# A small clear on GpSimd ahead of every gather of two graph convolutions

## The reference, cut to what matters

```python
def _gcn_conv(x, src, dst, W, b):
    ones = jnp.ones((src.shape[0],), x.dtype)
    deg_out = jnp.maximum(jax.ops.segment_sum(ones, src, num_segments=N), 1.0)
    deg_in = jnp.maximum(jax.ops.segment_sum(ones, dst, num_segments=N), 1.0)
    h = x * (deg_out ** (-0.5))[:, None]
    h = h @ W
    m = jax.ops.segment_sum(h[src], dst, num_segments=N)
    return m * (deg_in ** (-0.5))[:, None] + b

h = _gcn_conv(x, src, dst, W1, b1)
h = jax.nn.relu(h)
h = _gcn_conv(h, src, dst, W2, b2)
h = _layer_norm(h, gamma, beta)
```

## Time and profile before

| what | value |
|---|---|
| median of 3 runs | 5543.09 us (5528.74 to 5544.08) |
| span of the profiled execution, first to last instruction | 5492.7 us |
| median less that span | 50.4 us |
| busy share of the span: PE, PEld, DVE, ACT, POOL | 70%, 53%, 42%, 38%, 52% |
| mean granted TensorE clock | 0.822 of full speed |
| first convolution, first gather to last sum | 2793.8 to 4003.6 us |
| second convolution, first gather to last sum | 4074.4 to 5390.7 us |

### The profile page before, as it was taken

The page is one execution under the profiler, slowest core; times in us unless marked ns, Lnnn a source line. Parts: engine busy times, 40 slices in busy tenths (PEclk is TensorE's granted clock), DMA queues, the critical chain, the costliest instruction groups (busy, mean ns, idle before and its releaser), DMA issues. The chain is left out here.

```text
span 5492.7 us, 62308 instructions
## 1 busy us (share of the span) xinstructions
PE 3840.4 (70%) x14678; PEld 2895.6 (53%) x14678; DVE 2333.7 (42%) x6705; ACT 2062.8 (38%) x4818; POOL 2835.2 (52%) x2849
## 2 busy tenths in 40 slices
PE   4555577777769699999925555555566777777775
PEld 2333355555558588888813333333344555555554
DVE  7444455656546711111133233333354444444445
ACT  6333222222225522222243333333344555555552
POOL 2666655565540033333346666666626666666660
PEclk7776788889889899999957666777687888888987
DMA  3333466656568534444453333333323333333331
GB/s 106 103 108 105 142 190 188 197 176 203 186 211 278 180 104 108 113 113 107 97 164 97 98 96 97 98 98 98 96 89 92 90 91 89 88 89 89 90 89 57
DMA packets 329290, 674.18 MB, mean 123 GB/s; under 512 B 63069, under 2 KB 142237, under 8 KB 328812
## 3 DMA queue, kind: packets, MB, share of 16 engines
q0 software_dynamic: 146768, 365.78, 22.9%
q1 hardware_dynamic: 178716, 301.28, 18.1%
q10 hardware_dynamic: 3456, 3.15, 0.2%
HBM read 512.51 MB, written 165.30 MB: 123 GB/s over the span
## 5 line engine op out<-in xcount | busy, mean ns | idle before, releaser
L732 POOL DMA_INDIRECT messages<-work,small x880 | 888.4, 1010 | 637.1 <-ACT work L855 282.7
L782 POOL DMA_INDIRECT work<-conv_rows,tables x880 | 836.6, 951 | 549.2 <-issue 242.0
L2224 PE MATMUL bank<-work,reg_a 128*128 x1760 | 658.2, 523 | 604.9 <-issue 519.4
L772 POOL DMA_INDIRECT work<-conv_rows,tables x831 | 785.7, 946 | 448.6 <-issue 238.2
L2078 PE MATMUL bank<-reg_b,reg_a 128*128 x1760 | 580.0, 466 | 462.6 <-issue 219.3
L2224 PEld LDWEIGHTS bank<-work,reg_a 128*128 128x128 f32 x1760 | 416.2, 257 | 846.9 <-issue 786.3
L855 ACT ACTIVATE work<-bank,tables 128x256 f32<-128x256 f32 x880 | 399.3, 474 | 1083.8 <-PE bank L2078 672.1
L2370 PE MATMUL bank<-work,reg_a 128*128 128x256 f32 x1760 | 553.7, 442 | 285.2 <-DVE reg_b L1899 150.4
L1677 DVE TENSOR_TENSOR reg_b<-reg_b,bank 128x257 f32 x880 | 372.6, 423 | 837.3 <-remote 290.6
L2078 PEld LDWEIGHTS bank<-reg_b,reg_a 128*128 128x128 f32 x1760 | 356.1, 224 | 650.6 <-issue 612.1
L1899 DVE TENSOR_TENSOR reg_b<-reg_b,bank 128x256 f32 x880 | 371.3, 422 | 718.1 <-PE bank L2370 286.7
(11 more groups left out here) (457 smaller groups left out, 5304.1 us busy)
## 6 DMA issues: line engine op xcount, KB each, us to landing
reg_b<-messages SPq DMA_DIRECT2D x350, 258.0 KB
reg_a<-in_L_ffn_W_dram SPq DMA_DIRECT2D x56, 1024.0 KB
b_rows<-messages SPq DMA_DIRECT2D x116, 258.0 KB
reg_a<-item_rows SPq DMA_DIRECT2D x110, 256.0 KB
work<-conv_rows,tables POOLq DMA_INDIRECT x1711
work<-messages SPq DMA_DIRECT2D x98, 258.0 KB
messages<-work,small POOLq DMA_INDIRECT x880
conv_rows<-work SPq DMA_DIRECT2D x14, 896.0 KB, 4.1
```

The lines of the kernel that those rows point to most:

```text
L732: g.indirect_dma_start(msgs, bass.IndirectOffsetOnAxis(ap=PIDX[:, i % 32:i % 32 + 1], axis=0), G[:, u, :], None, bounds_check=BASES[2] + L ...
L772: g.indirect_dma_start(GC[:, u, 0:D], None, table, bass.IndirectOffsetOnAxis(ap=BSRC[:, b_:b_ + 1], axis=0)).then_inc(z(f"conv_in{u // 4}" ...
L782: g.indirect_dma_start(GC2[:, u, :], None, table, bass.IndirectOffsetOnAxis(ap=source_rank(i), axis=0)).then_inc(z(f"conv_in{u // 4}"), 16)
L2224: pe.matmul(ps[i % 8][:, 0:D + 1], OHP[:, i % OHR, :], GCf[:, bass.ds(offs[i % 4], D + 1)], start=True, stop=True).then_inc(z(f"{tag}_mm"), 1)
```

## The change

Ahead of each gather of both convolutions GpSimd now clears sixteen columns of `JUNK` and counts that in a new semaphore, `paced`. The clear itself waits until the clear of the gather before is complete. The gathers, their tables, their rings and their waits for free slots are the same, only that the wait for slots now stands with the clear.

```diff
@@ -769,6 +769,9 @@
                     u = b_ % UC
                     if b_ >= UC and b_ % 4 == 0:
                         pool.wait_ge(z(f"{tag}_free"), b_ - UC + 4)
+                    if b_:
+                        pool.wait_ge(z("paced"), b_)
+                    g.memset(JUNK[:, 0:16], 0.0).then_inc(z("paced"), 1)
                     g.indirect_dma_start(GC[:, u, 0:D], None, table,
                                          bass.IndirectOffsetOnAxis(ap=BSRC[:, b_:b_ + 1], axis=0)
                                          ).then_inc(z(f"conv_in{u // 4}"), 16)
@@ -779,6 +782,8 @@
                     u = i % U2
                     if i >= U2 and i % 4 == 0:
                         pool.wait_ge(z("p2_mm"), i - U2 + 4)
+                    pool.wait_ge(z("paced"), NBLK + i)
+                    g.memset(JUNK[:, 0:16], 0.0).then_inc(z("paced"), 1)
                     g.indirect_dma_start(GC2[:, u, :], None, table,
                                          bass.IndirectOffsetOnAxis(ap=source_rank(i), axis=0)
                                          ).then_inc(z(f"conv_in{u // 4}"), 16)
```

## The result

The changed kernel takes 5551.84 us (median of 20 runs, 5535.05 to 5573.52), the kernel before, beside it, 5538.88 us (20 runs, 5521.24 to 5555.96). The ratio is 1.0032, with a 95% interval of 1.0022 to 1.0042: slower by 0.3%, where 5503 us and faster were forecast. The time lies inside the range, on the other side of no change.

A forecast was written before the change was run, and what follows sets the result against it. Bound: a floor of about 1.44 us a gather. First convolution's start and end 5 us, second convolution 30, shorter stops 5: -40 from a span of 5492.7, plus 50.4 beyond it, gives 5503 us; range 5365 to 5680.

The forecast's parts named there:

- a floor: Both convolutions: gathers cannot average under about 1.44 us each, since unbroken runs leave work made up when POOL idles.
- others' sequencers are slow because of the runs: Both convolutions: unbroken gathers delay all engines' semaphore updates and sequencer steps, VectorE's from 0.02 to 0.05 us to 0.70.
- The price of the clear: POOL between two gathers: a sixteen-column clear adds 0.10 us, 171 us over 1711 if uncovered, but the pauses cover it.
- the debt: Work that unbroken gathers leave behind, some 0.19 us each; the new wait was to keep it near one gather's worth.
- the -30 us of the second convolution: Second convolution: 879 gathers go from 1.474 to 1.44 us each, saving 30 us.
- the 5 us of shorter stops: End of the second convolution and the hand-written order: shorter stops of the engines save 5 us.
- the forecast's own step of 1.35 us: POOL inside a run: the step from gather to gather becomes 1.35 us with a clear of 0.10 us.
- The slower rivals: POOL between gathers: the clear costs more than its cover, from 0.20 us on; 163 to 368 us more; chance 0.29.
- an added update that raises the floor: Within the slower case: one update more in seventeen lifts 1.44 us a gather to 1.53, about +125 us.
- No debt: Both convolutions: spaced gathers leave nothing behind, POOL's step of 1.35 us becomes the bound; 179 us less, 5364 us; chance 0.17.
- the own range: The forecast case, chance 0.35: floor 1.40 to 1.46 us, clear up to 0.19; -87 to -5 us, 5456 to 5538 us.

The follow-up runs named there:

- The rounds: Kernel before plus extra rounds of 192 gathers without consumer ahead of the first convolution, most beside a chain of small VectorE operations; held gathers step 1.40 us.
- the wide clears: The changed kernel with clears of 216 columns in place of sixteen, ahead of each gather: ratio 0.9996 to the kernel before; in the second convolution only, 0.9997.

## Why the prediction was wrong, point by point

- **That a mean of some 1.44 us a gather is a floor, made by the gathers and paid in pauses**: right in the main. With steps of 1.20, 1.25, 1.26, 1.28 and 1.41 us the first convolution's means were 1.455, 1.434, 1.462, 1.477 and 1.446, and the kernel before has 1.434 to 1.455 by itself; only at 1.49 does the step show. The rounds put the rate of the gathers at 1.40 us. What was missing is how it acts: for some 177 gathers in a row nothing holds GpSimd. The others are slowed after 13 or 14, and they stop GpSimd through the full ring. The 0.03 to 0.05 us between 1.40 and the means are not explained, and a pace of the consumers' own just under 1.44 is not excluded.
- **That others' sequencers are slow because of the runs**: right, and shown by the rounds; the wide clears agree.
- **The price of the clear**: 0.10 us was taken, with zero as the lower end, "part of the gap of 0.30 us may cover it". That end was the true one: 0.01 us a step. The rule of the Trainium skill, GPSIMD Engine Reference, Instruction dispatch, under which completion gates only what waits on the semaphore, pointed to the low end, and the trace agrees (clear right behind the gather, step 1.26).
- **The step that failed**: "So the debt stays near one gather's worth". I held that the wait makes GpSimd the victim of its own late update. It isn't late: in the stop at 4690 us clear follows clear on time, and in both stages together the wait cost 1.4 us of idle time. With a step of 1.26 us the runs are as dense as before, the backlog arises as before, and the -30 us of the second convolution (1.474 to 1.44) and the 5 us of shorter stops don't come. The mean was 1.499 instead, and the stops 140 us (111 before, up to 136 in unchanged stages). The wait was taken for a spacer, and it spaces nothing. A step of 1.41 us does give the even gathers that I had forecast. Even the forecast's own step of 1.35 us would have been 0.05 us a gather too fast for the 1.40 of the rounds.
- **And the gain would not have come with pacing**: with 1.41 us the stops shrink to 65 us, and the time is that of before. What is not lost in slow steps is spent at GpSimd's step, and PE's matmuls take 90 us more of the first convolution at a lower granted clock. The run with four empty instructions shows the same at a step of 1.27 us (PE busy for 772 us at 0.66, time +0.26%).
- **The slower rivals**: the direction was right and the mechanism was not. The clear's price never came near 0.20 us. What cost 0.3% was the handshake in dense runs: an added update that raises the floor was named there, and priced at about +125 us as one update more beside the 16 that the Trainium skill, DMA: Bandwidth & Descriptors, on why a DMA increments its semaphore by 16, gives a gather from GpSimd. Measured for one update more is +0.11% (-0.10 to +0.31), at most 17 us. No run counted the updates of a gather.
- **No debt** (-179 us) is out, and the mean step of a convolution never fell under 1.43 in any run.
- **Smaller slips**: a floor of 1.40 us gives 28 + 65 = 93 us from the two stages, not the 87 at the low end of the own range. And a count at one moment, 4600 us, shows the ring nearly full then, not "at all times". Neither decided anything.

Open: what the backlog is made of. No row names the path; the rounds show its rate, perhaps how much can be owed, and that bytes, PSUM and SBUF don't matter. One candidate was not tested: every execution here has a span and a clock from the profiler's records, so if writing such records is itself what is late, no run would tell. Why a handshake that never has to wait costs 0.2 to 0.3% in dense runs is not shown either.

## What to carry to other kernels

When an engine works in runs and pauses and its mean is far from its step, look for what the runs do to the others before speeding up or pacing it: a faster step (1.20 us) and a slower one (1.41 us) both ended at about the same mean here. A wait on one's own last instruction spaces nothing if that instruction fits in a gap that was there; to space, time must pass, and past the rate at which the backlog is worked off it costs (+0.48% at 1.49 us). Below that rate it bought no time either here. One profiled pair is thin evidence for a stage: the pair here showed 46 us in the two stages where the runs showed about 17. In such dense runs even an empty handshake is not free: 1711 of them cost 0.3%.

## What was not expected of the hardware

- A GpSimd clear of 128 x 16 takes 0.13 us and disappears in the 0.30 us between two gathers; one of 128 x 216 takes 0.29 and lengthens the step by 0.16.
- Dense gathers (one in 1.25 us) beside an engine with small dependent operations: after 13 or 14 gathers these go from one per 0.21 to 0.25 us to one per 1.40; after some 178 the gather itself goes from 0.95 to 1.10 us and from steps of 1.25 to 1.40; and the slowness lasts 26 to 27 us after the last of 192 gathers, with no data moving. At one gather in 1.41 us it begins only after 67 gathers and is weaker.
- 192 gathers with every other engine waiting run at 1.251 us each without a pause, the last of them taking 1.10 us.
- Small VectorE operations that fall on a GpSimd clear of 216 columns took 0.29 us in place of 0.18.
- With the holes in PE's work made smaller, the same 1760 matmuls of the first convolution kept PE busy for 748 us (clears of 216 columns) and 811 us (216 and 64) in place of 658, at granted clocks of 0.64 and 0.60 in place of 0.69.
- Waiting for a gather's landing on GpSimd cost 2.5 us from the end of its work to the next gather.
